# Column sums of a pairwise-product kernel on 64-row halves of the array, with the dense rows written behind the bank copies

## The chip, the cores and the metric

The kernel runs on one core of one Trainium2 chip. The metric is the device time of one execution in microseconds (us); lower is better. In the text PE is the matmul engine (PEld its weight loads), DVE the vector engine, ACT the scalar engine, POOL the engine that issues the gathers, SP the one that issues the other DMAs.

## What is computed

2048 samples each have 32 ids. Every id picks a row of 64 floats from its own table, which makes `e` of shape 2048 x 32 x 64. For each pair of fields i < j (496 pairs) there is a 64 x 64 matrix, and the value of the pair is a bilinear form; a small three-layer network follows, all in float32:

```python
p, q = x[:, row_idx, :], x[:, col_idx, :]          # row_idx, col_idx: the 496 pairs
z = einsum('bpe,fpe,bpf->bp', p, kernel, q)        # 2048 x 496
h = concatenate([z, dense_ctx], axis=1)            # 496 + 16 = 512 columns
h = maximum(h @ W_top1 + b_top1, 0)                # 512 -> 512
h = maximum(h @ W_top2 + b_top2, 0)                # 512 -> 256
y = h @ W_top3                                     # 256 -> 1
```

## The kernel before

The samples are taken in 4 chunks of 512. Within a chunk the samples lie along the free dimension, and the features of two fields (2 x 64) along the 128 partitions.

- **Gather and turn.** POOL gathers rows with indirect DMAs (line 181), 8 for a pair of fields, into a ring of four slots `rows`. PE transposes them (`turn`, line 218) into a side bank, and ACT copies them to `xt`.
- **Duos.** The 496 pairs are handled four at a time; such a group is a duo, 124 in a chunk. Of these 120 are "block" duos: two matmuls, each with a 64x128 weight tile on one half of the array's rows (`bilinear`, lines 270 and 271), which write the two banks of `y_ps`. Four duos of a chunk are "special" (pairs within one block) and use four 64x64 tiles (lines 273 to 276). DVE then multiplies the 128 x 1024 results by the other field's features and writes `products`, a ring of four (line 417).
- **Sums.** Two duos are a quad, 62 in a chunk. `add_up` (line 288) sums the products of a quad over features with a 0/1 matrix `selector` as weights: four matmuls, one per block of 32 output partitions. With the product of a duo's bank as moving operand, partitions 0 to 63 belong to one pair and 64 to 127 to another, so the selector has two columns of ones, and one matmul puts two rows into the bank. A bank of 128 rows (4 x 32) is full after 16 quads (`Z_QUADS`); there are four banks' worth in a chunk (`Z_BANKS`), which alternate between `sum_ps[0]` and `sum_ps[1]`. The last one has only 28 of every 32 rows filled (`SUM_ROWS`); the other 16 rows of `z_sb` hold the dense features.
- **Bank copies.** ACT copies a full bank to `z_sb` (`copy_bank`); the last one of a chunk goes in four copies of 28 rows, so that the dense rows are left alone. While ACT copies one bank, PE sums into the other.
- **Dense rows.** SP writes the dense rows with four DMAs of 4 rows (`place_dense`, line 197), for chunks 0 and 1 at the start, and for chunks 2 and 3 when layer 1 of the chunk that used the same half of `z_sb` is done.
- **Network.** `layer1` (line 231), `layer2` (239) and `layer3` (247) of chunk c are side jobs, placed between the duos of chunk c+1 by `side_schedule`: the first of the four `layer1` jobs stands before duo 6. For the last chunk they run alone behind the last sum.

PE takes its work in program order: side jobs that are due before a duo, the duo, and behind each odd duo the sum of the quad before. Each engine's program is written out by hand and synchronised by semaphores. A float32 matmul appears in the trace as two records (passes), each with a weight load of its own.

The sum before, as it stands in `add_up`:

```python
for m in range(4):
    last = nc.tensor.matmul(sum_ps[kb % 2][32 * m:32 * m + 32, :], selector[:, 30 - 2 * s:62 - 2 * s],
                            products[:, (2 * g + m // 2) % 4, m % 2, :], ...)
```

Of the kernel before, what the change touches and what calls it, by code (L numbers as in the profile page):

```python
# [10 lines left out]
B, F, E = 2048, 32, 64  # L11
DENSE, H1, H2 = 16, 512, 256
P = 128
N = 512
CHUNKS = B // N
# [21 lines left out]
QUADS = DUOS // 2  # L37
FIRST_DUO = {q: DUO.index(("block", 0, q)) for q in range(1, PAIRS)}
SPECIAL_DUO = {u: DUO.index(("special", u, None)) for u in range(SPECIALS)}

Z_QUADS = P // 8
Z_BANKS = -(-QUADS // Z_QUADS)
SUM_ROWS = 2 * (QUADS - (Z_BANKS - 1) * Z_QUADS)

PIECES = [(0, 4)] + [(d, d + 8) for d in range(4, DUOS, 8)]

# [13 lines left out]
def z_rows():  # L60
    rows, dense = [], 0
    for kb in range(Z_BANKS):
        for r in range(P):
            column_tile, s, half = r // 32, r % 32 // 2, r % 2
            quad = kb * Z_QUADS + s
            if quad < QUADS:
                duo = DUO[2 * quad + column_tile // 2]
                rows.append(tuple(sorted(field_pair(duo, column_tile % 2, half))))
            else:
                rows.append(dense)  # L70
                dense += 1
    return rows
# [29 lines left out]
SIDE = {job: k for k, job in enumerate(SIDE_ORDER)}  # L102


def dlrm_tower(nc, ids, tables, pair_kernel, dense, w1, b1, w2, b2, w3, out):
    with ExitStack() as ctx:  # L106
        def psum(name, shape):
            return ctx.enter_context(nc.psum_tensor(name, shape, F32))

        def sem(name):  # L110
            return ctx.enter_context(nc.semaphore(name))

        def sb(name, shape, dt=F32):
            return ctx.enter_context(nc.sbuf_tensor(name, shape, dt))
# [5 lines left out]
        products = sb("products", [P, 4, 2, N])  # L120
        z_sb = sb("z_sb", [P, 2, Z_BANKS, N])
        w1_sb = sb("w1_sb", [P, 4, H1])
# [6 lines left out]
        y_sb = sb("y_sb", [P, N])  # L129
        idx = sb("idx", [P, CHUNKS, TILES, F], I32)  # L130
        identity = sb("identity", [P, P])
        selector = sb("selector", [P, 62])

        y_ps = [psum(f"y_ps{i}", [P, 2, N]) for i in range(2)]
        sum_ps = [psum(f"sum_ps{i}", [P, N]) for i in range(2)]
# [7 lines left out]
        selector_made = sem("selector_made")  # L143
        kernel_landed = [sem(f"kernel_landed{i}") for i in range(len(PIECES))]
        weights_landed = sem("weights_landed")
        dense_landed = [sem(f"dense_landed{c}") for c in range(CHUNKS)]
        side_ready = sem("side_ready")
# [4 lines left out]
        quad_summed = sem("quad_summed")  # L152
        bank_kept = sem("bank_kept")
        out_written = sem("out_written")

        LAST_BANK = Z_BANKS - 1

        def banks_kept(c, kb):

            return c * (Z_BANKS + 3) + (kb + 1 if kb < LAST_BANK else Z_BANKS + 3)  # L160

        block = ctx.enter_context(nc.Block())

# [21 lines left out]
        @block.sync  # L185
        def _(sp):
            sp.dma_start(idx[:, 0], ids[:, 0]).then_inc(ids_landed[0], 16)
            for p, (lo, hi) in enumerate(PIECES):
                sp.dma_start(kernel_sb[:, lo:hi, :], pair_kernel[:, lo:hi, :]).then_inc(kernel_landed[p], 16)
                if p == 3:  # L190
                    sp.dma_start(idx[:, 1:], ids[:, 1:]).then_inc(ids_landed[1], 16)
            for dst, src in ((w1_sb, w1), (w2_sb, w2), (w3_sb, w3), (b1_sb, b1), (b2_sb, b2)):
                sp.dma_start(dst[:], src).then_inc(weights_landed, 16)

            def place_dense(c):
                for g in range(4):
                    sp.dma_start(z_sb[32 * g + SUM_ROWS:32 * g + 32, c % 2, LAST_BANK, :],
                                 dense[4 * g:4 * g + 4, c * N:c * N + N]).then_inc(dense_landed[c], 16)

            place_dense(0)  # L200
            place_dense(1)
            for c in range(CHUNKS):
                if c + 2 < CHUNKS:
                    sp.wait_ge(side_ready, SIDE["layer1", c, 3] + 1)
                    place_dense(c + 2)
                sp.wait_ge(side_kept, SIDE["layer3", c, 0] + 1)
                sp.dma_start(out[:, c * N:c * N + N], y_sb[32 * c:32 * c + 1, :]).then_inc(out_written, 16)
            sp.wait_ge(out_written, CHUNKS * 16)

        @block.tensor  # L210
        def _(pe):
# [10 lines left out]
            def layer1(c, n):  # L222
                k = SIDE["layer1", c, n]
                if n == 0:
                    pe.wait_ge(bank_kept, banks_kept(c, LAST_BANK))
                    pe.wait_ge(dense_landed[c], 4 * 16)
                    if c == 0:
                        pe.wait_ge(weights_landed, 5 * 16)
                pe.wait_ge(side_kept, k - 1)
                for kb in range(4):  # L230
                    last = nc.tensor.matmul(side_ps[k % 2][:], w1_sb[:, kb, n * P:n * P + P], z_sb[:, c % 2, kb, :],  # L231
                                            start=(kb == 0), stop=(kb == 3))
                last.then_inc(side_ready, 1)
# [46 lines left out]
            def add_up(c, quad):  # L280
                g = c * QUADS + quad
                pe.wait_ge(duo_multiplied, 2 * g + 2)
                kb, s = quad // Z_QUADS, quad % Z_QUADS
                if s == 0 and c * Z_BANKS + kb >= 2:
                    free = c * Z_BANKS + kb - 2
                    pe.wait_ge(bank_kept, banks_kept(free // Z_BANKS, free % Z_BANKS))
                for m in range(4):
                    last = nc.tensor.matmul(sum_ps[kb % 2][32 * m:32 * m + 32, :], selector[:, 30 - 2 * s:62 - 2 * s],  # L288
                                            products[:, (2 * g + m // 2) % 4, m % 2, :],
                                            start=(s == 0), stop=(s == Z_QUADS - 1 or quad == QUADS - 1))  # L290
                last.then_inc(quad_summed, 1)

            pe.wait_ge(identity_made, 1)
            pe.wait_ge(selector_made, 2)
            for c in range(CHUNKS):
                stored, pieces = 0, 0
                for d in range(DUOS):
                    for job in SIDE_BEFORE[c, d]:
                        side(job)
                    kind, s, q = DUO[d]  # L300
# [17 lines left out]
        def _(act):  # L318
            def copy(dst, src):
                return nc.scalar.activation(dst, src, ACT.Copy)  # L320
# [47 lines left out]
                copy(special[high, u % 2, 0, :], x[high, 4 * u + 2, :]).then_inc(special_kept, 1)  # L368
                copy(special[low, u % 2, 0, :], x[high, 4 * u + 3, :]).then_inc(special_kept, 1)

            def copy_bank(c, kb):
                act.wait_ge(quad_summed, c * QUADS + min(Z_QUADS * (kb + 1), QUADS))
                if c >= 2 and kb == 0:
                    act.wait_ge(side_ready, SIDE["layer1", c - 2, 3] + 1)
                if kb < LAST_BANK:
                    copy(z_sb[:, c % 2, kb, :], sum_ps[kb % 2][:]).then_inc(bank_kept, 1)
                else:
                    for g in range(4):
                        part = slice(32 * g, 32 * g + SUM_ROWS)
                        copy(z_sb[part, c % 2, kb, :], sum_ps[kb % 2][part, :]).then_inc(bank_kept, 1)  # L380

            for c in range(CHUNKS):
                for d in range(DUOS):
                    for job in SIDE_BEFORE[c, d]:
                        keep(job)
                        if c == 0 and job[0] == "turn" and job[1] == 0 and job[2] % 4 == 3:
                            special_slots(0, job[2] // 4)
                    for u in range(SPECIALS):
                        if c and d == max(0, SPECIAL_DUO[u] - 14):
                            special_slots(c, u)  # L390
                    if d % 2 and d > 2 and (d // 2) % Z_QUADS == 0:
                        copy_bank(c, d // 2 // Z_QUADS - 1)
                    if d == 1 and c:
                        copy_bank(c - 1, LAST_BANK)
            copy_bank(CHUNKS - 1, LAST_BANK)
            for job in SIDE_AFTER:
                keep(job)

        @block.vector
        def _(dve):  # L400
            nc.vector.memset(selector[:], 0.0).then_inc(selector_cleared, 1)
            dve.wait_ge(selector_cleared, 1)
            nc.vector.memset(selector[0:E, 30:31], 1.0).then_inc(selector_made, 1)
            nc.vector.memset(selector[E:P, 31:32], 1.0).then_inc(selector_made, 1)
            for c in range(CHUNKS):
                for d in range(DUOS):
                    g = c * DUOS + d
                    if g >= 4:
                        dve.wait_ge(quad_summed, g // 2 - 1)
                    dve.wait_ge(duo_ready, g + 1)  # L410
                    kind, s, q = DUO[d]
                    if kind == "block":
                        by = xt[:, c % 2, s, :].unsqueeze(1).to_broadcast([P, 2, N])
                    else:
                        dve.wait_ge(special_kept, 4 * (c * SPECIALS + s + 1))
                        by = special[:, s % 2]
                    nc.vector.tensor_tensor(products[:, g % 4], y_ps[g % 2][:], by, ALU.mult).then_inc(duo_multiplied, 1)  # L417
# [45 lines left out]
```

## Time and profile before

| | |
|---|---|
| median of 3 runs | 920.45 us (918.14 to 920.97) |
| profiled execution | 919.69 us, span 917.9 us |
| busy: PE / DVE / POOL / ACT | 94% / 64% / 53% / 12% of the span |
| mean granted clock of TensorE | 0.994 |
| HBM read | 26.91 MB, mean 29 GB/s |
| DVE multiplies | 496 x 1.22 us |
| PE records: y 64x128, sums 128x32 | 1920, 1984 |

The span runs from the first to the last instruction of the profiled execution, whose own time is 1.8 us longer. Busy shares say which engine is full, not what ends the work; for that the waits and the timeline are read. Matmul ends in the trace are modelled and overlap with the next start, so phases of PE are read from start to start. Times of the timeline count from the span's start.

### The profile page before, as it was taken

To read this page: it belongs to the slowest core of one execution; us is meant where nothing else is said; L and a number is where in the kernel's file an instruction comes from. 1 tells how busy PE (TensorE), PEld (TensorE's weight loads), DVE (VectorE), ACT (ScalarE), POOL (GpSimd) and SP (SyncE) were. 2 spreads that over 40 slices of the span, in tenths; PEclk is the share of its full clock that TensorE was granted. 3 is DMA by queue.
4 is the path that set the end of the run, shared out by engine and by line. 5 is a ranking of instruction groups with operands and counts; after the bars stand their busy time and mean duration, and the time that the engine had idled before them with its cause. 6 is when DMAs were issued, how large, how long until landed. Compare 5 with 4: busy or idle time off the path is not lost.

```text
span 917.9 us, 10931 instructions
## 1 busy us (share of the span) xinstructions
PE 864.0 (94%) x4496; PEld 272.8 (30%) x4496; DVE 584.5 (64%) x499; ACT 114.3 (12%) x185; POOL 483.9 (53%) x518
## 2 busy tenths in 40 slices
PE   0189999999999999999999999999999999999988
PEld 0123333332333332333233333333333333222223
DVE  0047777777746558777765656777776566778840
ACT  0011011100211111101112011001111110100012
POOL 6777777777777776677535465567724600000000
PEclk9989999999999999999999999999999999999999
DMA  9411111111111111111100011111100100000000
GB/s 338 148 27 27 28 27 26 28 27 27 27 27 28 28 26 24 24 25 25 21 12 19 18 24 19 21 25 25 25 9 18 22 2 1 0 1 1 1 0 0
DMA packets 19881, 27.64 MB, mean 30 GB/s; under 512 B 9012, under 2 KB 9268, under 8 KB 19704
## 3 DMA queue, kind: packets, MB, share of 16 engines
q0 software_dynamic: 16384, 16.81, 9.4%
q1 hardware_dynamic: 3448, 10.14, 3.0%
q8 instruction: 35, 0.57, 0.3%
q14 instruction: 14, 0.11, 0.0%
HBM read 26.91 MB, written 0.01 MB: 29 GB/s over the span
## 4 chain that ended last, share of the span: by engine, by line
PE 71%; POOL 20%; issue 7%; DMA 0%; ACT 0%; DVEq 0%; DVE 0%; POOLq 0%
PE y_ps L270 37%; POOL rows L181 20%; PE sum_ps L288 20%; PE side_ps L231 6%; PE side_ps L239 3%; PE side_ps L218 3%; PE y_ps L273 1%; PE side_ps L247 1%; PE y_ps L271 1%; DMA rows<-tbl_dram,idx 0%; ACT z_sb L320 0%; DMA idx<-ids_dram 0%; DVEq L106 0%; DVE products L417 0%; ACT h_sb L340 0%
## 5 line engine op out<-in xcount | busy, mean ns | idle before, releaser
L417 DVE TENSOR_TENSOR products<-y_ps,xt 128x1024 f32<-128x1024 f32 x480 | 566.1, 1219 | 281.3 <-PE y_ps L271 281.2
L181 POOL DMA_INDIRECT rows<-tbl_dram,idx x512 | 483.2, 944 | 249.4 <-issue 150.1
L270 PE MATMUL y_ps<-xt,kernel_sb 64*128 64x512 f32 x960 | 481.1, 620 | 0.5 <-DVE products L417 0.4
L271 PE MATMUL y_ps<-xt,kernel_sb 64*128 64x512 f32 x960 | 481.2, 620 | 0.0
L288 PE MATMUL sum_ps<-products,selector 128*32 128x512 f32 x1984 | 264.2, 605 | 0.7 <-DVE products L417 0.7
L270 PEld LDWEIGHTS y_ps<-xt,kernel_sb 64*128 64x128 f32 x960 | 160.2, 187 | 286.8 <-DVE products L417 182.9
L271 PEld LDWEIGHTS y_ps<-xt,kernel_sb 64*128 64x128 f32 x960 | 159.9, 187 | 0.0
L320 ACT ACTIVATE xt<-side_ps 128x512 f32<-128x512 f32 x64 | 38.2, 597 | 503.7 <-PE side_ps L218 479.4
L288 PEld LDWEIGHTS sum_ps<-products,selector 128*32 128x32 f32 x1984 | 39.1, 108 | 189.1 <-issue 187.6
L218 PE MATMUL side_ps<-identity,rows 128*128 128x128 f32 x256 | 44.7, 300 | 46.4 <-DMA rows<-tbl_dram,idx 46.4
L231 PE MATMUL side_ps<-z_sb,w_sb 128*128 128x512 f32 x128 | 59.5, 613 | 2.5 <-ACT z_sb L320 2.5
L218 PEld LDWEIGHTS side_ps<-identity,rows 128*128 128x128 f32 x256 | 28.5, 147 | 98.2 <-issue 60.3
L320 ACT ACTIVATE special<-xt 64x512 f32<-64x512 f32 x64 | 40.1, 627 | 1.6
L320 ACT ACTIVATE z_sb<-sum_ps 28x512 f32<-28x512 f32 (+1 forms) x28 | 16.6, 592 | 190.4 <-PE sum_ps L288 190.1
L231 PEld LDWEIGHTS side_ps<-z_sb,w_sb 128*128 128x128 f32 x128 | 23.9, 195 | 34.0 <-issue 30.5
L417 DVE TENSOR_TENSOR products<-y_ps,special 128x1024 f32<-128x1024 f32 x16 | 19.6, 1222 | 19.1 <-issue 19.1
L239 PE MATMUL side_ps<-h_sb,w_sb 128*128 128x512 f32 x64 | 29.3, 604 | 0.8 <-ACT h_sb L334 0.8
L334 ACT ACTIVATE h_sb<-side_ps,b_sb 128x512 f32<-128x512 f32 x16 | 11.0, 687 | 66.5 <-PE side_ps L231 66.5
L239 PEld LDWEIGHTS side_ps<-h_sb,w_sb 128*128 128x128 f32 x64 | 11.6, 190 | 18.6 <-issue 17.0
L276 PE MATMUL y_ps<-xt,kernel_sb 64*64 64x512 f32 x32 | 17.1, 615 | 0.0
L273 PE MATMUL y_ps<-xt,kernel_sb 64*64 64x512 f32 x32 | 17.1, 615 | 0.0
L274 PE MATMUL y_ps<-xt,kernel_sb 64*64 64x512 f32 x32 | 17.1, 615 | 0.0
(19 smaller groups left out, 48.4 us busy)
## 6 DMA issues: line engine op xcount, KB each, us to landing
rows<-tbl_dram,idx POOLq DMA_INDIRECT x512, 2.4
kernel_sb<-pair_kernel_dram SPq DMA_DIRECT2D x15, 512.0 KB, 11.0
w_sb<-w_dram SPq DMA_DIRECT2D x1, 1024.0 KB, 18.2
w_sb<-w_dram SPq DMA_DIRECT2D x1, 512.0 KB, 18.1
kernel_sb<-pair_kernel_dram SPq DMA_DIRECT2D x1, 256.0 KB, 2.8
z_sb<-dense_dram SPq DMA_DIRECT2D x16, 8.0 KB
idx<-ids_dram SPq DMA_DIRECT2D x1, 192.0 KB, 6.9
idx<-ids_dram SPq DMA_DIRECT2D x1, 64.0 KB, 1.9
```

The source lines that it names most:

```text
L181: pool.indirect_dma_start(rows[:, slot, t, h, :], None, tables[j], bass.IndirectOffsetOnAxis(ap=idx[:, c, t, j:j + 1], axis=0)).then_inc(r ...
L218: last = nc.tensor.transpose(side_ps[k % 2][:, t * P:(t + 1) * P], rows[:, q % ROW_RING, t].rearrange("p h e -> p (h e)"), identity[:])
L231: last = nc.tensor.matmul(side_ps[k % 2][:], w1_sb[:, kb, n * P:n * P + P], z_sb[:, c % 2, kb, :], start=(kb == 0), stop=(kb == 3))
L239: last = nc.tensor.matmul(side_ps[k % 2][:], w2_sb[:, kb, n * P:n * P + P], h1_sb[:, kb, :], start=(kb == 0), stop=(kb == 3))
L270: nc.tensor.matmul(y[:, 0, :], kernel_sb[low, d, :], x[low, q, :], start=True, stop=True)
L271: last = nc.tensor.matmul(y[:, 1, :], kernel_sb[high, d, :], x[high, q, :], start=True, stop=True)
L273: nc.tensor.matmul(y[low, 0, :], kernel_sb[low, d, low], x[low, 4 * s + 3, :], start=True, stop=True)
L274: nc.tensor.matmul(y[low, 1, :], kernel_sb[high, d, low], x[high, 4 * s, :], start=True, stop=True)
L276: last = nc.tensor.matmul(y[high, 1, :], kernel_sb[high, d, high], x[high, 4 * s + 1, :], start=True, stop=True)
L288: last = nc.tensor.matmul(sum_ps[kb % 2][32 * m:32 * m + 32, :], selector[:, 30 - 2 * s:62 - 2 * s], products[:, (2 * g + m // 2) % 4, m % ...
L320: return nc.scalar.activation(dst, src, ACT.Copy)
L417: nc.vector.tensor_tensor(products[:, g % 4], y_ps[g % 2][:], by, ALU.mult).then_inc(duo_multiplied, 1)
```

## The change

Each matmul of the sum is split in two along the rows: partitions 0 to 63 and 64 to 127 are separate 64x32 tiles, each with one column of ones, and each half of the rows has a bank of its own (`sum_ps[half]`). A quad now takes eight matmuls, and a pair of banks fills over 32 quads (`Z_QUADS = P // 4`). Both banks of a pair are copied together, by two whole copies, and the first sum of the next pair waits for both. In a chunk's last pair 30 of every 32 rows are sums. The copies now cover all 128 rows, so the dense rows can only be written behind them: SP waits until all copies of the chunk are done and then issues eight DMAs of 2 rows; `layer1` waits for these. The rows of the first weight matrix are permuted on the host to match.

```diff
-Z_QUADS = P // 8
-Z_BANKS = -(-QUADS // Z_QUADS)
-SUM_ROWS = 2 * (QUADS - (Z_BANKS - 1) * Z_QUADS)
+Z_QUADS = P // 4
+Z_BANKS = 2 * -(-QUADS // Z_QUADS)
+SUM_ROWS = QUADS % Z_QUADS
...
-            def place_dense(c):
-                for g in range(4):
-                    sp.dma_start(z_sb[32 * g + SUM_ROWS:32 * g + 32, c % 2, LAST_BANK, :],
-                                 dense[4 * g:4 * g + 4, c * N:c * N + N]).then_inc(dense_landed[c], 16)
-
-            place_dense(0)
-            place_dense(1)
             for c in range(CHUNKS):
-                if c + 2 < CHUNKS:
-                    sp.wait_ge(side_ready, SIDE["layer1", c, 3] + 1)
-                    place_dense(c + 2)
+                sp.wait_ge(bank_kept, (c + 1) * Z_BANKS)
+                for kb in range(Z_BANKS - 2, Z_BANKS):
+                    for g in range(4):
+                        row = 8 * (kb - Z_BANKS + 2) + 2 * g
+                        sp.dma_start(z_sb[32 * g + SUM_ROWS:32 * g + 32, c % 2, kb, :],
+                                     dense[row:row + 2, c * N:c * N + N]).then_inc(dense_landed[c], 16)
...
                 if n == 0:
-                    pe.wait_ge(bank_kept, banks_kept(c, LAST_BANK))
-                    pe.wait_ge(dense_landed[c], 4 * 16)
+                    pe.wait_ge(dense_landed[c], 8 * 16)
...
-                kb, s = quad // Z_QUADS, quad % Z_QUADS
-                if s == 0 and c * Z_BANKS + kb >= 2:
-                    free = c * Z_BANKS + kb - 2
-                    pe.wait_ge(bank_kept, banks_kept(free // Z_BANKS, free % Z_BANKS))
+                kb, s = quad // Z_QUADS * 2, quad % Z_QUADS
+                if s == 0 and c * Z_BANKS + kb:
+                    pe.wait_ge(bank_kept, c * Z_BANKS + kb)
                 for m in range(4):
-                    last = nc.tensor.matmul(sum_ps[kb % 2][32 * m:32 * m + 32, :], selector[:, 30 - 2 * s:62 - 2 * s],
-                                            products[:, (2 * g + m // 2) % 4, m % 2, :],
-                                            start=(s == 0), stop=(s == Z_QUADS - 1 or quad == QUADS - 1))
+                    for half in range(2):
+                        part = slice(half * E, half * E + E)
+                        last = nc.tensor.matmul(sum_ps[half][32 * m:32 * m + 32, :], selector[part, 31 - s:63 - s],
+                                                products[part, (2 * g + m // 2) % 4, m % 2, :],
+                                                start=(s == 0), stop=(s == Z_QUADS - 1 or quad == QUADS - 1))
                 last.then_inc(quad_summed, 1)
...
-                if kb < LAST_BANK:
-                    copy(z_sb[:, c % 2, kb, :], sum_ps[kb % 2][:]).then_inc(bank_kept, 1)
-                else:
-                    for g in range(4):
-                        part = slice(32 * g, 32 * g + SUM_ROWS)
-                        copy(z_sb[part, c % 2, kb, :], sum_ps[kb % 2][part, :]).then_inc(bank_kept, 1)
+                for half in range(2):
+                    copy(z_sb[:, c % 2, kb + half, :], sum_ps[half][:]).then_inc(bank_kept, 1)
...
-            nc.vector.memset(selector[0:E, 30:31], 1.0).then_inc(selector_made, 1)
-            nc.vector.memset(selector[E:P, 31:32], 1.0).then_inc(selector_made, 1)
+            nc.vector.memset(selector[:, 31:32], 1.0).then_inc(selector_made, 1)
```

How the instructions stand now. On PE, in one quad of chunk 1 (y matmuls of two duos, then the sum), before:

```order
L270 MATMUL y_ps<-xt,kernel_sb 128x512 [waits duo_multiplied]
L271 MATMUL y_ps<-xt,kernel_sb 128x512
L270 MATMUL y_ps<-xt,kernel_sb 128x512 [waits duo_multiplied]
L271 MATMUL y_ps<-xt,kernel_sb 128x512
L288 MATMUL sum_ps<-products,selector 32x512 [waits duo_multiplied]
L288 MATMUL sum_ps<-products,selector 32x512 x3
```

and after:

```order
L259 MATMUL y_ps<-xt,kernel_sb 128x512 [waits duo_multiplied]
L260 MATMUL y_ps<-xt,kernel_sb 128x512
L259 MATMUL y_ps<-xt,kernel_sb 128x512 [waits duo_multiplied]
L260 MATMUL y_ps<-xt,kernel_sb 128x512
L278 MATMUL sum_ps<-products,selector 32x512 [waits duo_multiplied]
L278 MATMUL sum_ps<-products,selector 32x512 x7
```

The order is the same; the sum has eight matmuls in place of four.

On SP, behind the weights, before:

```order
L197 DMA z_sb<-dense_dram 4x512 x8
L197 DMA z_sb<-dense_dram 4x512 [waits side_ready]
L197 DMA z_sb<-dense_dram 4x512 x3
L207 DMA out_dram<-y_sb 1x512 [waits side_kept]
```

and after:

```order
L194 DMA z_sb<-dense_dram 2x512 [waits bank_kept]
L194 DMA z_sb<-dense_dram 2x512 x7
L197 DMA out_dram<-y_sb 1x512 [waits side_kept]
L194 DMA z_sb<-dense_dram 2x512 [waits bank_kept]
L194 DMA z_sb<-dense_dram 2x512 x7
```

Each chunk has eight issues, and they stand behind that chunk's bank copies.

On ACT, at the end of the program, before:

```order
L320 ACTIVATE special<-xt 64x512 x3
L320 ACTIVATE z_sb<-sum_ps 28x512 [waits quad_summed]
L320 ACTIVATE z_sb<-sum_ps 28x512 x3
L334 ACTIVATE h_sb<-side_ps,b_sb 128x512 [waits side_ready] x4
```

and after:

```order
L310 ACTIVATE special<-xt 64x512 x3
L310 ACTIVATE z_sb<-sum_ps 128x512 [waits quad_summed]
L310 ACTIVATE z_sb<-sum_ps 128x512
L324 ACTIVATE h_sb<-side_ps,b_sb 128x512 [waits side_ready] x4
```

Two whole copies stand where four of 28 rows stood.

## Rows read from the trace of the kernel before

**Rows 1.** The page: busy time by engine, us (share of the span) xinstructions.
```profile
PE 864.0 (94%) x4496; PEld 272.8 (30%) x4496; DVE 584.5 (64%) x499; ACT 114.3 (12%) x185; POOL 483.9 (53%) x518
```

**Rows 2.** Waits of PE, then POOL, 75 to 254 us: total, times, longest.
```profile
PE side_ps L218 <- DMA rows<-tbl_dram,idx: 1.5, 2, 0.9
POOL rows L181 <- issue: 44.2, 145, 0.3
```

**Rows 3.** Waits of PE from 258 us to the end.
```profile
PE side_ps L231 <- ACT z_sb L320: 2.5, 1, 2.5
PE side_ps L247 <- ACT h_sb L340: 0.8, 1, 0.8
PE side_ps L239 <- ACT h_sb L334: 0.8, 1, 0.8
PE sum_ps L288 <- DVE products L417: 0.7, 1, 0.7
```

**Rows 4.** Timeline, 502 to 505 us: start, us, engine, line, operation.
```profile
502.24 0.59 PE L270 MATMUL y_ps<-xt,kernel_sb 64*128 64x512 f32 x1
...
502.76 1.07 PE L288 MATMUL sum_ps<-products,selector 128*32 128x512 f32 x8
503.76 0.18 PEld L270 LDWEIGHTS y_ps<-xt,kernel_sb 64*128 64x128 f32 x1 [0.84 <-DVE products L417]
...
504.29 0.59 PE L270 MATMUL y_ps<-xt,kernel_sb 64*128 64x512 f32 x1
...
504.72 0.59 PE L270 MATMUL y_ps<-xt,kernel_sb 64*128 64x512 f32 x1
```

**Rows 5.** Timeline, 306 to 308 us, around a special duo.
```profile
306.09 0.59 PE L271 MATMUL y_ps<-xt,kernel_sb 64*128 64x512 f32 x1
...
306.60 0.13 PEld L273 LDWEIGHTS y_ps<-xt,kernel_sb 64*64 64x64 f32 x1 [0.76 <-DVE products L417]
...
306.66 0.13 PEld L273 LDWEIGHTS y_ps<-xt,kernel_sb 64*64 64x64 f32 x1
...
306.68 0.13 PEld L276 LDWEIGHTS y_ps<-xt,kernel_sb 64*64 64x64 f32 x1
...
307.62 0.16 PEld L288 LDWEIGHTS sum_ps<-products,selector 128*32 128x32 f32 x8 [0.81 <-issue]
```

**Rows 6.** Line 288 by stretch: its length, PE busy (records), PEld busy (records), clock.
```profile
254.00:886.90 632.90, 197.11 (x1480) 29.16 (x1480) 1.00 0.09 17
75.00:254.00 179.00, 61.02 (x460) 8.99 (x456) 1.00 0.14 27
```

**Rows 7.** Timeline of the end.
```profile
886.97 2.42 ACT L320 ACTIVATE z_sb<-sum_ps 28x512 f32<-28x512 f32 x4 [36.56 <-PE sum_ps L288]
...
889.44 15.70 PE L231 MATMUL side_ps<-z_sb,w_sb 128*128 128x512 f32 x32 [2.54 <-ACT z_sb L320]
```

**Rows 8.** Timeline where chunk 1 ends, 465 to 472 us.
```profile
465.06 2.43 ACT L320 ACTIVATE z_sb<-sum_ps 28x512 f32<-28x512 f32 x4 [20.29 <-PE sum_ps L288]
...
466.84 1.07 PE L288 MATMUL sum_ps<-products,selector 128*32 128x512 f32 x8
...
471.33 1.55 PE L231 MATMUL side_ps<-z_sb,w_sb 128*128 128x512 f32 x3
```

**Rows 9.** Timeline of SP's issues: four dense pieces, and the last output.
```profile
299.82 1.26 SPq L197 DMA_DIRECT2D z_sb<-dense_dram  x4
...
916.38 0.23 SPq L207 DMA_DIRECT2D out_dram<-y_sb  x1
```

**Rows 10.** The page: DMA issues, KB each, us from issue to landing.
```profile
kernel_sb<-pair_kernel_dram SPq DMA_DIRECT2D x1, 256.0 KB, 2.8
...
idx<-ids_dram SPq DMA_DIRECT2D x1, 64.0 KB, 1.9
```

**Rows 11.** All engines by stretch at the end, with the granted clock.
```profile
890.40:893.80 3.40, 3.40 (x5) 1.33 (x4) 0.00 (x0) 0.00 (x0) 0.00 (x0) 0.50 0.00 0
893.80:918.00 24.20, 20.38 (x47) 8.09 (x45) 0.00 (x0) 4.71 (x7) 0.00 (x0) 1.00 0.00 0
```

More of the change, by code:

```diff
@@ L63, in z_rows @@
         for r in range(P):
-            column_tile, s, half = r // 32, r % 32 // 2, r % 2
-            quad = kb * Z_QUADS + s
+            column_tile, s, half = r // 32, r % 32, kb % 2
+            quad = kb // 2 * Z_QUADS + s
             if quad < QUADS:
@@ L131, in dlrm_tower @@
         identity = sb("identity", [P, P])
-        selector = sb("selector", [P, 62])
+        selector = sb("selector", [P, 63])
         y_ps = [psum(f"y_ps{i}", [P, 2, N]) for i in range(2)]
@@ L154, in dlrm_tower @@
         out_written = sem("out_written")
-        LAST_BANK = Z_BANKS - 1
-        def banks_kept(c, kb):
-            return c * (Z_BANKS + 3) + (kb + 1 if kb < LAST_BANK else Z_BANKS + 3)
         block = ctx.enter_context(nc.Block())
@@ L282, in add_up @@
                 pe.wait_ge(duo_multiplied, 2 * g + 2)
-                kb, s = quad // Z_QUADS, quad % Z_QUADS
-                if s == 0 and c * Z_BANKS + kb >= 2:
-                    free = c * Z_BANKS + kb - 2
-                    pe.wait_ge(bank_kept, banks_kept(free // Z_BANKS, free % Z_BANKS))
+                kb, s = quad // Z_QUADS * 2, quad % Z_QUADS
+                if s == 0 and c * Z_BANKS + kb:
+                    pe.wait_ge(bank_kept, c * Z_BANKS + kb)
                 for m in range(4):
-                    last = nc.tensor.matmul(sum_ps[kb % 2][32 * m:32 * m + 32, :], selector[:, 30 - 2 * s:62 - 2 * s],
-                                            products[:, (2 * g + m // 2) % 4, m % 2, :],
-                                            start=(s == 0), stop=(s == Z_QUADS - 1 or quad == QUADS - 1))
+                    for half in range(2):
[3 more added lines that the diff above has]
+                                                start=(s == 0), stop=(s == Z_QUADS - 1 or quad == QUADS - 1))
                 last.then_inc(quad_summed, 1)
             pe.wait_ge(identity_made, 1)
-            pe.wait_ge(selector_made, 2)
+            pe.wait_ge(selector_made, 1)
             for c in range(CHUNKS):
@@ L369, in special_slots, with copy_banks @@
                 copy(special[low, u % 2, 0, :], x[high, 4 * u + 3, :]).then_inc(special_kept, 1)
-            def copy_bank(c, kb):
-                act.wait_ge(quad_summed, c * QUADS + min(Z_QUADS * (kb + 1), QUADS))
+            def copy_banks(c, kb):
+                act.wait_ge(quad_summed, c * QUADS + min(Z_QUADS * (kb // 2 + 1), QUADS))
                 if c >= 2 and kb == 0:
                     act.wait_ge(side_ready, SIDE["layer1", c - 2, 3] + 1)
-                if kb < LAST_BANK:
-                    copy(z_sb[:, c % 2, kb, :], sum_ps[kb % 2][:]).then_inc(bank_kept, 1)
-                else:
-                    for g in range(4):
-                        part = slice(32 * g, 32 * g + SUM_ROWS)
-                        copy(z_sb[part, c % 2, kb, :], sum_ps[kb % 2][part, :]).then_inc(bank_kept, 1)
+                for half in range(2):
+                    copy(z_sb[:, c % 2, kb + half, :], sum_ps[half][:]).then_inc(bank_kept, 1)
             for c in range(CHUNKS):
@@ L391, in _ @@
                     if d % 2 and d > 2 and (d // 2) % Z_QUADS == 0:
-                        copy_bank(c, d // 2 // Z_QUADS - 1)
+                        copy_banks(c, 2 * (d // 2 // Z_QUADS - 1))
                     if d == 1 and c:
-                        copy_bank(c - 1, LAST_BANK)
-            copy_bank(CHUNKS - 1, LAST_BANK)
+                        copy_banks(c - 1, Z_BANKS - 2)
+            copy_banks(CHUNKS - 1, Z_BANKS - 2)
             for job in SIDE_AFTER:
```

## The prediction

> **What bounds the kernel now.** I read the page's busy shares first: PE is busy for 94% of the span, DVE for 64%, ACT for 12% [rows 1]. A busy share alone does not say who sets the end, so the next view is who waited for whom, cut at the point where the kinds of wait change. From 75 to 254 us PE waits 1.5 us in all, both times in a turn for gathered rows, while POOL waits for nobody but its own issue [rows 2]: in this stretch the gather sets the pace and PE keeps just behind it. From 258 us on PE waits for another engine only four times, 4.8 us in all, and all of it in the last 33 us [rows 3]. So every microsecond that is added to PE's stream between 254 and 887 us is a microsecond of the time, and what is added before 254 us is partly eaten by the 1.5 us of waiting.
>
> Next the timeline of one quad of the steady state [rows 4]. Starts are 0.43 us apart while y matmuls follow each other (504.29 and 504.72). From the last y start at 502.24 to the first sum start it is 0.52, and from the last sum start (first at 502.76, and the phase is over at 503.76) again some 0.52. So the array is empty for about 0.09 us at each change of the tile's form, and the first weight load behind it is not hidden. The whole sum phase, from its first weight load to the next y's, takes 503.76 - 502.76 = 1.00 us, of which two passes are 2 x 0.43 = 0.86.
>
> Is it the change from 64-row to 128-row tiles that empties the array? Four duos of a chunk are "special": 64x64 tiles between 64x128 ones and sums. There the row height stays at 64 and only the columns change, and from the last 64x128 start (306.09) to the first 64x64 load (306.60) it is 0.51 to 0.52 us, as everywhere else [rows 5]. So a change of columns alone already costs the same gap. After the edit the sums are 64x32 between 64x128 tiles: the column width still changes. I expect both gaps to stay.
>
> **The change part by part.** (a) *Eight matmuls for four in each quad.* The sum of a quad moves the same columns: all 128 rows and all 128 columns of the array are covered by eight 64x32 tiles as by four 128x32. If the eight run side by side, the two passes stay 0.86 us. What grows is the stagger: in the special duo the first of the four second loads starts at 306.66 and the fourth at 306.68, so one start takes about 0.02/3 = 0.0067 us [rows 5]. The phase ends with the last tile, hence four more starts add 4 x 0.0067 = 0.027 us to a quad. A check on the same rows: the special phase (four tiles, 64-column load) is 307.62 - 306.60 = 1.02 against 1.00 for the sum (four tiles, 32-column load of half the length), so phases are the sum of load, two passes, stagger and gap. From 254 us to the end 1480 sum records are 185 quads of eight [rows 6]; the very last one waits 0.7 us for DVE anyway [rows 3], which leaves 184. 184 x 0.027 = **+4.9 us**. In the stretch before 254 us 460 records are 57 quads, 57 x 0.027 = 1.5, as much as the 1.5 us that PE waits there for rows [rows 2, 6]: nothing. The rows are rounded to 0.01, which leaves 0.005 to 0.008 us a start and 3.7 to 5.9 for the term. It is 0 if the starts hide behind the pass; its upper bound is that only four tiles run at a time: one more pass of 0.43 a quad (a rival below).
> In a sentence of its own: the Trainium skill, page "TensorE: Matmul & The Clock Gate", section "Measured speedup vs the span model", has a pack's span as one matmul plus about 4 ns for each further tile; by that the term would be 184 x 4 x 0.004 = 2.9 us, an estimate. The row of this trace (6.7 ns) is the one I use.
>
> (b) *Bank hand-over.* Before, bank k is copied while the other one fills. Now both banks of a pair fill together and the next quad must wait for both copies. At a chunk's end the four copies of today begin at 465.06, take 2.43 together, so 0.61 each, and the next sum starts at 466.84 [rows 8]; two copies end at 465.06 + 1.21 = 466.27. Spare: 0.57 us, seven times in the kernel, and ACT (12% busy) has nothing else due there: **0**. If that cover were gone, it would be at most 7 x 0.6 = 4 us.
>
> (c) *Dense rows behind the copies.* Three of the four chunks have cover. SP may issue from 466.27 on. One issue of a 4-row piece takes 1.26/4, hence with the pause between two about 0.33 us [rows 9]; eight are 7 x 0.33 = 2.3. The landing of such a small one has no time in the trace; the 64 KB load of the indices lands after 1.9, the 256 KB piece of the kernel after 2.8, and the 2 KB output ends the program 917.9 - 916.38 = 1.5 after its issue at most [rows 9, 10]. I take 1.8, near the larger. Then the dense rows are there at 466.3 + 2.3 + 1.8 = 470.4, and layer 1 starts at 471.33 [rows 8]: 0.9 us spare, **0**. If it fails, PE stands and with it the duos queued behind layer 1: 3 times up to about 1 us.
> The last chunk has no cover. Now: ACT starts at 886.97, four copies of 28 rows take 2.42, layer 1 begins at 889.44 [rows 7]. After: two copies end at 886.97 + 1.21 = 888.18, the last of eight issues is at +2.3 = 890.5, landed at +1.8 = 892.3. Layer 1 at 892.35 in place of 889.44: **+2.9 us**. Bounds: landing 1.5 to 2.8, an issue 0.25 to 0.4, so +2.0 to +4.4.
>
> (d) *PE's clock at the end.* After today's 2.54 us of idle PE [rows 7] the granted clock falls to 0.50 from 890.4 to 893.8, and is 1.00 again after it [rows 11]; that stretch of 3.4 us costs 1.7 us. After the edit the idle stretch is 5.5 us. The half clock may then fall partly into the idle time (cheaper) or last longer (dearer). I book **0**, with -1.0 to +1.7 as bounds.
>
> (e) *The small ones.* Copies go from 28 to 16 and the first eight dense writes leave SP's start, where no one waited for them; the selector is one memset fewer; PE reads 992 more matmul instructions, and its queue was ahead, since the four starts of a pack follow at 0.0067. All 0. On SP the dense writes of a chunk now stand behind the output of the chunk before, which follows layer 3 before duo 46, long before the copies at the chunk's end.
>
> Sum: 4.9 + 0 + 0 + 2.9 + 0 = +7.8 us against the profiled execution (919.69, span 917.9): 927.5. The median of the runs shown, 920.45, is 0.8 above the profiled one, so the forecast is **928.0**.
>
> **The rivals.**
> *A, only four tiles at a time* (chance 0.08). No row shows more than four tiles side by side: y has two, special and sum four. If the fifth has to wait for a second pass to begin, a quad takes one pass more, 0.43 us: 184 x 0.43 = 79, plus 57 x 0.43 - 1.5 = 23 before 254 us, plus 2.9, on 920.45: about 1025 us. Against it speaks that four tiles in a 2 by 2 arrangement behave like four in a row [rows 5]. The Trainium skill, same page, section "Measured speedup vs the span model", lists sixteen 32x32 tiles at once; no run here shows it.
> *B, faster: the gap is tied to row height after all* (0.03). It is one mechanism, at both ends of each sum: without a change of rows the array would not be emptied, and a quad would save 2 x 0.09 of gap plus the exposed load (the first two starts of y are 504.29 - 503.76 = 0.53 apart, 0.10 over a pass [rows 4]) = 0.28. It decides as soon as it exceeds (7.8/184) = 0.04 a quad. 184 x 0.28 = 52 less, with the tail's 2.9 more: 872 us; POOL would not stop it, it waits for PE from 254 us on. Against it speaks the 0.51 at the special duo [rows 5].
> *C, nothing measurable* (0.05): the starts hide, the tail costs 2 us or the clock falls into the idle time: 920.5 to 923.
> *D, the covers of (b) or (c) are too thin* (0.09): as forecast plus 3 to 6 us, 931 to 934.
>
> **How the numbers follow.** The forecast has 0.75. Its own range: term (a) 3.7 to 5.9, tail 2.0 to 4.4, clock -1.0 to +1.7, all against 920.45, gives 925 to 932. With D and part of C the range 922 to 935 holds the time in 8 to 9 of 10 cases; rival A and B stay out. A measurement of this kernel tells about 0.3% (2.8 us) from no change, that is 917.7 to 923.2. Slower by more: forecast, A, D = 0.92. Within: C = 0.05. Faster: B = 0.03.
>
> **What would show it.** In the profile after: 3968 records of 64x32 sums with starts some 7 ns apart, all eight first passes before any second one; a sum phase of 1.02 to 1.03 us in place of 1.00; the gaps of 0.52 unchanged; no PE wait for ACT at the first sum of a pair; one PE wait of 5 to 6 us before the last layer 1, with a DMA as what ended it, and eight issues on SP inside it. The prediction is wrong if the sum phase is near 1.4 us (A) or under 0.95 us (B), or if PE waits for z_sb at the chunks' borders (D).

## The result, and the profile after

The changed kernel takes 927.45 us (median of 4 runs, 927.07 to 930.25) against 920.31 for the kernel before on the same chip; the ratio is 1.0088, 95% interval 1.0062 to 1.0114. It is 7.1 us slower. The forecast was 928.0, range 922 to 935.

The profiled execution of the changed kernel is the longest of its four, 930.25 us with a span of 928.5, so 2.8 us above the median; where it differs from the others is told below. First a steady quad, from the timeline (start, us, engine, line, operation); it answers to [rows 4]:

```profile
507.07 0.59 PE L260 MATMUL y_ps<-xt,kernel_sb 64*128 64x512 f32 x1
...
507.59 0.18 PEld L278 LDWEIGHTS sum_ps<-products,selector 64*32 64x32 f32 x16 [0.76 <-issue]
507.59 1.09 PE L278 MATMUL sum_ps<-products,selector 64*32 64x512 f32 x16
508.61 0.18 PEld L259 LDWEIGHTS y_ps<-xt,kernel_sb 64*128 64x128 f32 x1 [0.84 <-DVE products L402]
```

All sixteen records of a sum lie within 1.09 us, so eight tiles run side by side: a quad has no third or fourth pass. The phase from the first sum load to the next y load is 508.61 - 507.59 = 1.02 us against 1.00. The gap ahead of it (from the last y start to the first sum start) is 507.59 - 507.07 = 0.52 as before.

Single rows are rounded to 0.01 us, too coarse for 0.02 a quad. The starts of the first layer 1 job in chunks 2 and 3 are 62 quads apart, with the same side jobs between them in both kernels, and serve as marks. Here they are from PE's timeline, first of the kernel before:

```profile
471.33 1.13 PE L231 MATMUL side_ps<-z_sb,w_sb 128*128 128x512 f32 x2
...
685.22 1.13 PE L231 MATMUL side_ps<-z_sb,w_sb 128*128 128x512 f32 x2
```

and of the changed one:

```profile
476.02 0.70 PE L220 MATMUL side_ps<-z_sb,w_sb 128*128 128x512 f32 x1
...
691.37 1.12 PE L220 MATMUL side_ps<-z_sb,w_sb 128*128 128x512 f32 x2
```

That is 213.89 against 215.35 us: 1.46 more for 62 quads, 0.0235 us a quad. Over the 184 quads that PE paces it makes 4.3 us. The figure repeats: the profiles of the three kernels with the old sums (before, runs 2 and 7) have 213.89 us, those of the six with eight tiles (after, runs 1, 4, 5, 6 and 8) 215.33 to 215.35.

In the nanoseconds that the traces hold, the starts of a sum's tiles follow each other by 6.7 ns on average in both kernels. Four more of them are 27 ns. The gap behind the sum, from its last start to the next y start, is 4 ns shorter (519 in place of 523 ns, medians over the steady stretch), which leaves 23. Ahead of the sum it is 518 to 520 ns in both.

Where a chunk ends, the timeline of the changed kernel answers to [rows 8]:

```profile
469.74 1.08 ACT L310 ACTIVATE z_sb<-sum_ps 128x512 f32<-128x512 f32 x2 [20.52 <-PE sum_ps L278]
...
470.85 2.31 SPq L194 DMA_DIRECT2D z_sb<-dense_dram  x8
...
471.48 1.09 PE L278 MATMUL sum_ps<-products,selector 64*32 64x512 f32 x16
```

The two copies are done at 470.82, 0.66 us before the first sum of the next pair, and the eight issues at 473.16, 2.9 us before layer 1 at 476.02 (the second fence of marks). PE waits for neither. What PE waits for from 256 us on (total, times, longest) shows that the dense rows cost something in one place alone; it answers to [rows 3]:

```profile
PE side_ps L220 <- DMA z_sb<-dense_dram: 4.7, 1, 4.7
PE side_ps L228 <- ACT h_sb L324: 0.8, 1, 0.8
PE side_ps L236 <- ACT h_sb L330: 0.8, 1, 0.8
PE sum_ps L278 <- DVE products L402: 0.7, 1, 0.7
```

And the end, from the timeline and from the table by stretch (length, busy time of PE, PEld, DVE, ACT, POOL with their records, then the granted clock), which answer to [rows 7, 11]:

```profile
894.54 1.08 ACT L310 ACTIVATE z_sb<-sum_ps 128x512 f32<-128x512 f32 x2 [83.54 <-PE sum_ps L278]
895.65 2.31 SPq L194 DMA_DIRECT2D z_sb<-dense_dram  x8
...
899.17 9.23 PE L220 MATMUL side_ps<-z_sb,w_sb 128*128 128x512 f32 x15 [4.73 <-DMA z_sb<-dense_dram]
```

```profile
897.40:904.20 6.80, 5.03 (x6) 2.19 (x7) 0.00 (x0) 0.00 (x0) 0.00 (x0) 0.50 0.02 3
904.40:928.00 23.60, 20.33 (x47) 8.05 (x45) 0.00 (x0) 4.71 (x7) 0.00 (x0) 1.00 0.00 0
255.80:259.10 3.30, 3.30 (x12) 1.42 (x10) 0.54 (x1) 0.60 (x1) 2.40 (x3) 0.50 0.13 27
```

ACT's first copy starts 4.63 us before layer 1 (899.17 - 894.54) against 2.47 before (889.44 - 886.97): +2.2 us. The half clock now lasts 6.8 us, of which PE works 5.0; before it was 3.4 with PE at work all the time. So it costs 2.5 in place of 1.7 us. From the start of layer 1 to the end of the span it is 29.3 us here and 28.5 before, and 26.8 in runs 1 and 8, whose clock stays up. The last row is a half clock of its own in the middle, right behind a wait for gathered rows:

```profile
255.51 0.93 PE L208 MATMUL side_ps<-identity,rows 128*128 128x128 f32 x4 [1.89 <-DMA rows<-tbl_dram,idx]
```

The kernel before waited 0.58 us at that turn and its clock stayed up. In the profiled runs of the other kernels with these sums (waits of at most 1.5 us there) the clock stays up too. The half clock costs 1.7 us, and the longer wait 1.3. Together they are about the profiled execution's surplus over its median; the other three executions have no trace, but run 4, which does the same work, reaches this layer 1 at 257.60 in place of 260.67 and takes 926.92 us.

The account of that profile: +3.2 us until the first layer 1 (257.45 before, 260.67 after: the gather's longer wait and the half clock behind it), +1.46 a chunk for two chunks, +1.4 for the 60 quads from the last of these marks to ACT's copies (894.54 - 691.37 against 886.97 - 685.22), +2.2 from ACT's first copy to layer 1, +0.9 in the clock. Together 10.6, the difference of the spans.

### The profile page after: what moved, and what is told of

It reads as the page before. It is cut to its first block, busy times and chain, and to the rows that moved or that the text cites. A ratio compares the mean times of both kernels' runs of the same rounds, so it can differ in the third digit from the quotient of the medians.

```text
span 928.5 us, 14894 instructions
## 1 busy us (share of the span) xinstructions
PE 870.9 (94%) x6480; PEld 279.0 (30%) x6480; DVE 585.3 (63%) x498; ACT 106.4 (11%) x173; POOL 483.9 (52%) x518
## 4 chain that ended last, share of the span: by engine, by line
PE 71%; POOL 20%; issue 7%; DMA 1%; ACT 0%; SPq 0%; DVEq 0%; DVE 0%; POOLq 0%
PE y_ps L259 36%; POOL rows L175 20%; PE sum_ps L278 20%; PE side_ps L220 6%; PE side_ps L228 3%; PE side_ps L208 3%; PE y_ps L262 1%; PE side_ps L236 1%; PE y_ps L260 1%; DMA rows<-tbl_dram,idx 0%; DMA idx<-ids_dram 0%; SPq L194 0%; DVEq L106 0%; DMA z_sb<-dense_dram 0%; ACT z_sb L310 0%
## 5 line engine op out<-in xcount | busy, mean ns | idle before, releaser
L278 PE MATMUL sum_ps<-products,selector 64*32 64x512 f32 x3968 | 270.2, 601 | 0.7 <-DVE products L402 0.7
L278 PEld LDWEIGHTS sum_ps<-products,selector 64*32 64x32 f32 x3968 | 45.0, 105 | 189.4 <-issue 187.8
L228 PE MATMUL side_ps<-h_sb,w_sb 128*128 128x512 f32 x64 | 29.3, 604 | 0.8 <-ACT h_sb L324 0.8
L310 ACT ACTIVATE z_sb<-sum_ps 128x512 f32<-128x512 f32 x16 | 8.7, 595 | 163.7 <-PE sum_ps L278 163.7
```

The lines of the kernel that those rows point to most:

```text
L228: last = nc.tensor.matmul(side_ps[k % 2][:], w2_sb[:, kb, n * P:n * P + P], h1_sb[:, kb, :], start=(kb == 0), stop=(kb == 3))
L278: last = nc.tensor.matmul(sum_ps[half][32 * m:32 * m + 32, :], selector[part, 31 - s:63 - s], products[part, (2 * g + m // 2) % 4, m % 2, ...
```

## The experiments

Theory S is the forecast: four more starts in each sum on the stretch that PE paces, and the dense writes behind the last copies, with the clock. Theory T puts the whole loss at the end. Each ratio is against the kernel before on the same chip; a difference between two changed kernels is one of medians that can come from different chips, and is read together with the traces.

**1. Without the dense writes.**

```diff
-                sp.wait_ge(bank_kept, (c + 1) * Z_BANKS)
-                for kb in range(Z_BANKS - 2, Z_BANKS):
...
-                        sp.dma_start(z_sb[32 * g + SUM_ROWS:32 * g + 32, c % 2, kb, :],
-                                     dense[row:row + 2, c * N:c * N + N]).then_inc(dense_landed[c], 16)
...
-                    pe.wait_ge(dense_landed[c], 8 * 16)
+                    pe.wait_ge(bank_kept, (c + 1) * Z_BANKS)
```

> The changed kernel without its dense writes; layer 1 waits for the bank copies alone (the 16 dense columns are left out of the network's input). Theory S (my forecast: four more starts in each sum, 23 ns a quad on the stretch that PE sets, and the dense writes behind the last copies): the end loses the DMA wait, 5.3 us from the last sum's start to layer 1 becomes about 2, and the clock falls for a shorter time; time near 923, that is still 3 us above the kernel before. Theory T (the sums are free, the whole loss is the tail and the clock behind it): 919 or less. Sum phases stay 1.02 us under S.

Measured: 922.05 us, ratio 1.0030 (1.0018 to 1.0042). The wait at the end (PE's waits and timeline) is short:

```profile
PE side_ps L214 <- ACT z_sb L304: 1.2, 1, 1.2
```

```profile
890.82 1.09 PE L272 MATMUL sum_ps<-products,selector 64*32 64x512 f32 x16 [0.65 <-DVE products L396]
892.01 1.08 ACT L304 ACTIVATE z_sb<-sum_ps 128x512 f32<-128x512 f32 x2 [83.53 <-PE sum_ps L272]
...
893.15 2.41 PE L214 MATMUL side_ps<-z_sb,w_sb 128*128 128x512 f32 x5 [1.24 <-ACT z_sb L304]
```

The table by stretch has the clock at full to the end; it was expected to fall for a shorter time:

```profile
893.00:919.00 26.00, 23.04 (x52) 9.31 (x52) 0.00 (x0) 4.81 (x8) 0.00 (x0) 1.00 0.00 0
```

So the late dense rows are worth about 5.4 us of the changed kernel's 7.1. Left are 2.2 us against the kernel before, although two copies are now faster than four (1.3 us less wait) and the clock does not fall at the end (1.7 less). So something costs 5.2 us: the sums 4.3 by the marks (the chunk is 215.35 us here too), and in this profile the part ahead of the first layer 1 is 0.7 longer, where the three profiles with the old sums differ by 1.3 among themselves. Theory T, with 919 or less, falls.

**2. The dense rows late, the sums as before.** `place_dense` issues eight DMAs of 2 rows here.

```diff
-            place_dense(0)
-            place_dense(1)
...
             for c in range(CHUNKS):
...
+                sp.wait_ge(bank_kept, (c + 1) * Z_BANKS)
+                place_dense(c)
...
-                if kb < LAST_BANK:
-                    copy(z_sb[:, c % 2, kb, :], sum_ps[kb % 2][:]).then_inc(bank_kept, 1)
-                else:
...
+                copy(z_sb[:, c % 2, kb, :], sum_ps[kb % 2][:]).then_inc(bank_kept, 1)
```

> The kernel before with four 128x32 sums, but its last bank copied whole and the dense rows written behind the copy by eight DMAs of 2 rows. Theory S: stretches between the chunks' first layer 1 starts stay 213.9 us; from the last sum's start to layer 1 it grows from 3.1 to about 4.7 us (one copy less than in the changed kernel, the same eight issues); time 922 to 923.5. Theory T: the same loss as in the changed kernel, 927. If the dense writes have cover everywhere: 919, since three copies fewer stand in the tail.

Measured: 922.25 us, ratio 1.0026 (1.0012 to 1.0040), as S has it. The marks of chunks 2 and 3 and the end, from the timeline:

```profile
472.11 1.13 PE L230 MATMUL side_ps<-z_sb,w_sb 128*128 128x512 f32 x2
...
685.99 0.70 PE L230 MATMUL side_ps<-z_sb,w_sb 128*128 128x512 f32 x1
...
887.74 0.60 ACT L319 ACTIVATE z_sb<-sum_ps 128x512 f32<-128x512 f32 x1 [36.56 <-PE sum_ps L287]
888.36 2.31 SPq L199 DMA_DIRECT2D z_sb<-dense_dram  x8
...
892.01 1.96 PE L230 MATMUL side_ps<-z_sb,w_sb 128*128 128x512 f32 x2 [4.34 <-issue]
```

The chunk is back at 213.88 us with the old sums. Runs 1 and 2 thus each hold one part of the loss, and the chunk's length follows the sums, not the place of the dense writes. From ACT's copy to layer 1 it is 4.27 us, 1.8 more than before (from the first start of the last sum it is 5.4 against 3.6; the 4.7 and 3.1 of the expectation are counted from some 0.5 us later). The half clock behind this wait lasts 3.4 us, as in the kernel before, and not 6.8 as in the changed one.

**3. Sums in the form of the y matmuls.**

```diff
-                        last = nc.tensor.matmul(sum_ps[half][32 * m:32 * m + 32, :], selector[part, 31 - s:63 - s],
+                        at = 127 - 32 * m - s
+                        last = nc.tensor.matmul(sum_ps[half][:], selector[part, at:at + P],
                                                 products[part, (2 * g + m // 2) % 4, m % 2, :],
-                                                start=(s == 0), stop=(s == Z_QUADS - 1 or quad == QUADS - 1))
+                                                start=(s == 0 and m == 0),
+                                                stop=(m == 3 and (s == Z_QUADS - 1 or quad == QUADS - 1))
```

> The changed kernel with each sum in 64x128 tiles, the form of the y matmuls: the four column blocks run one behind the other through a 255-column selector, so a sum takes four times its passes (8 x 0.43 = 3.4 us) and the time is near 1450. Looked at for the gap alone. If the gap comes from the change of the tile's form, the last y start and the first sum start are 0.43 us apart and the first weight load is hidden. If it comes from the change of bank, from accumulation or from the wait on DVE, it stays at 0.52.

Measured: one run, 1483.7 us, where near 1450 was expected; the difference was not followed up. The 16 records of a quad's sum take 3.60 us. The timeline at a border of y and sum:

```profile
503.12 0.59 PE L259 MATMUL y_ps<-xt,kernel_sb 64*128 64x512 f32 x1
503.12 0.19 PEld L279 LDWEIGHTS sum_ps<-products,selector 64*128 64x128 f32 x2 [0.23 <-issue]
503.12 0.59 PE L260 MATMUL y_ps<-xt,kernel_sb 64*128 64x512 f32 x1
...
503.55 3.60 PE L279 MATMUL sum_ps<-products,selector 64*128 64x512 f32 x16
```

The sum starts 0.43 us behind the last y, and its weights are loaded during that y pass (503.12). The banks, the accumulation and the semaphore are as in the changed kernel; the form of the tile is equal now (and with it only two tiles run side by side), and the gap is gone, behind the sum too. So it is the change of form that empties the array. That tells why the edit could not gain: 64x128 to 64x32 is such a change as much as 64x128 to 128x32.

A change of rows alone has a price of its own. It stands in the trace of the kernel before, where the last pass of a layer 1 job (128x128) is followed by a y matmul (64x128) that waits for nobody:

```profile
500.32 0.59 PE L231 MATMUL side_ps<-z_sb,w_sb 128*128 128x512 f32 x1
500.84 0.69 PE L270 MATMUL y_ps<-xt,kernel_sb 64*128 64x512 f32 x1
```

That is 0.52 us again. So columns alone (the special duos), rows alone, and both together cost the same 0.09 us, to within 4 ns: 519 ns from start to start behind 64-row tiles, 522 or 523 behind 128-row ones.

**4. The other order of the eight.**

```diff
-                for m in range(4):
-                    for half in range(2):
+                for half in range(2):
+                    for m in range(4):
```

> The changed kernel with the eight matmuls of a sum in another order: four column blocks of the lower rows, then four of the upper ones. Theory S (tiles run side by side, only the starts are in line): no difference, 927, the eighth start 0.05 us behind the first. If row halves pair up, or if two tiles of one column block hold each other: a sum phase away from 1.02 us and a time away by more than 3 us.

Measured: 927.28 us, ratio 1.0090 (1.0074 to 1.0106), the same as the changed kernel. The marks of chunks 2 and 3:

```profile
472.94 1.13 PE L220 MATMUL side_ps<-z_sb,w_sb 128*128 128x512 f32 x2
...
688.27 0.70 PE L220 MATMUL side_ps<-z_sb,w_sb 128*128 128x512 f32 x1
```

215.33 us: the tiles do not disturb each other in either order.

**5. Dense issues on two queues.** ACT issues four of the eight behind its copies.

```diff
-                for kb in range(Z_BANKS - 2, Z_BANKS):
+                for kb in range(Z_BANKS - 2, Z_BANKS - 1):
...
+                if kb == Z_BANKS - 2:
+                    act.wait_ge(bank_kept, (c + 1) * Z_BANKS)
+                    for g in range(4):
+                        act.dma_start(z_sb[32 * g + SUM_ROWS:32 * g + 32, c % 2, Z_BANKS - 1, :],
+                                      dense[8 + 2 * g:10 + 2 * g, c * N:c * N + N]).then_inc(dense_landed[c], 16)
```

> The changed kernel with the eight dense issues split: SP issues four, ACT the other four behind its own copies. If the eight issues in line on SP are part of the tail (0.34 us each), the wait before the last layer 1 shrinks by about 4 x 0.34 = 1.3 us, to near 3.4, and the time by 1 to 3 us (the clock goes with it). If only the landing counts, the wait stays 4.7.

Measured: 926.41 us, ratio 1.0071 (1.0057 to 1.0085). SP's and ACT's issues and the wait:

```profile
893.75 1.12 SPq L194 DMA_DIRECT2D z_sb<-dense_dram  x4
893.75 1.23 ACTq L370 DMA_DIRECT2D z_sb<-dense_dram  x4
...
896.44 9.09 PE L220 MATMUL side_ps<-z_sb,w_sb 128*128 128x512 f32 x15 [3.91 <-DMA z_sb<-dense_dram]
```

The issues take half the time (1.2 for 2.31), and the wait shrinks by 0.8 of the expected 1.3 us. Part of the miss is the price of an issue: eight in line start 0.30 us apart, not 0.34, so four of them are worth 1.2. The median is 1.0 us lower, which the two intervals do not tell from nothing; the wait in the trace is the firmer figure. The half clock stays (0.50 from 894.5 to 901.2). Why another 0.3 us of the saving comes back in the landing is not settled; 1.5 us pass from the end of the issues to layer 1 here, 1.2 in the changed kernel.

**6. Layer 1 starts with its finished banks, in the changed kernel.**

```diff
                 if n == 0:
-                    pe.wait_ge(dense_landed[c], 8 * 16)
+                    pe.wait_ge(bank_kept, c * Z_BANKS + 2)
...
                 for kb in range(4):
+                    if n == 0 and kb == 2:
+                        pe.wait_ge(dense_landed[c], 8 * 16)
```

> The changed kernel, but layer 1 begins with the two banks that were copied 30 quads earlier and waits for the dense writes only before its third one. Two of the four weight blocks (2 x 0.86 = 1.7 us) then run inside the wait. Theory S (the tail is a plain wait on PE): 1.7 us less, and more if the clock stays up for longer; 924 to 926. If the wait only moves behind the two blocks and the clock falls as before: 926. If it were not the wait that costs: 927.

Measured: 924.47 us, ratio 1.0045 (1.0030 to 1.0059). The wait is 3.0 in place of 4.7 us, just the two blocks less, in the timeline of the end; the half clock lasts 3.4 in place of 6.8 us (the second fence, the table by stretch). From the last sum's start to the end of the span it is 2.4 us less than in the changed kernel; the other 0.6 of the 3.0 between the medians lies in the spread of the runs.

```profile
891.93 1.98 PE L222 MATMUL side_ps<-z_sb,w_sb 128*128 128x512 f32 x4
...
896.87 6.68 PE L222 MATMUL side_ps<-z_sb,w_sb 128*128 128x512 f32 x11 [2.95 <-DMA z_sb<-dense_dram]
```

```profile
897.20:900.60 3.40, 3.40 (x5) 1.35 (x4) 0.00 (x0) 0.20 (x1) 0.00 (x0) 0.50 0.00 0
900.70:922.00 21.30, 19.19 (x44) 7.50 (x42) 0.00 (x0) 4.34 (x7) 0.00 (x0) 1.00 0.00 0
```

**7. The same in the kernel before.** Layer 1 waits for its last bank only before the fourth block.

```diff
-                    pe.wait_ge(bank_kept, banks_kept(c, LAST_BANK))
-                    pe.wait_ge(dense_landed[c], 4 * 16)
+                    pe.wait_ge(bank_kept, banks_kept(c, LAST_BANK - 1))
...
                 for kb in range(4):
+                    if n == 0 and kb == LAST_BANK:
+                        pe.wait_ge(bank_kept, banks_kept(c, LAST_BANK))
+                        pe.wait_ge(dense_landed[c], 4 * 16)
```

> The kernel before with the same idea: layer 1 starts with its three finished banks and waits for the last one before the fourth block. 3 x 0.86 = 2.6 us of work cover the 2.5 us wait for ACT's four copies, and the clock has no idle stretch to fall behind. Time 920.3 - 2.5 - 1.7 = 916, under both kernels. If the clock falls all the same: 917.8.

Measured: 916.65 us, ratio 0.9960 (0.9946 to 0.9975). It beats both kernels. The end in its timeline, and its clock by stretch:

```profile
887.10 1.07 PE L290 MATMUL sum_ps<-products,selector 128*32 128x512 f32 x8 [0.67 <-DVE products L419]
...
888.10 9.32 PE L233 MATMUL side_ps<-z_sb,w_sb 128*128 128x512 f32 x21
888.24 2.42 ACT L322 ACTIVATE z_sb<-sum_ps 28x512 f32<-28x512 f32 x4 [36.56 <-PE sum_ps L290]
```

```profile
885.00:914.00 29.00, 25.50 (x71) 9.54 (x68) 2.05 (x2) 7.06 (x11) 0.00 (x0) 1.00 0.00 0
```

Layer 1 follows the last sum without a wait while ACT copies, and the granted clock is 1.00 throughout. Expected were 916. In the two profiles the part from the last sum's start to the end is 4.3 us shorter, as expected; the medians are 3.3 apart, and the first layer 1 is 1.3 us later in this profile.

**8. The wait filled with work of no use.**

```diff
             add_up(CHUNKS - 1, QUADS - 1)
+            for _ in range(5):
+                nc.tensor.matmul(y_ps[0][:, 0, :], w1_sb[:, 0, 0:P], w1_sb[:, 1, :], start=True, stop=True)
```

> The changed kernel with five 128x512 matmuls of no use (into a y bank that nobody reads any more) in the wait before the last layer 1; they take 5 x 0.86 = 4.3 us, less than the wait. If the idle time of PE is what lets the clock fall, the granted clock stays 1.00 to the end and the time drops by what the half clock costs behind the wait, 0.9 to 2.6 us, to 925 to 926.5. If the clock falls for another reason, 927 to 928.

Measured: 925.16 us, ratio 1.0061 (1.0047 to 1.0076), 2.3 us under the changed kernel.

```profile
891.16 4.56 PE L305 MATMUL y_ps<-w_sb 128*128 128x512 f32 x10
...
895.91 6.28 PE L220 MATMUL side_ps<-z_sb,w_sb 128*128 128x512 f32 x14 [0.18 <-DMA z_sb<-dense_dram]
```

```profile
888.00:922.00 34.00, 30.11 (x98) 11.49 (x94) 2.08 (x2) 5.80 (x9) 0.00 (x0) 1.00 0.01 2
```

The dense rows come no sooner, but the clock stays at 1.00. From the start of layer 1 to the end of the span it is 26.8 us in place of 29.3 (899.17 to 928.5), just the 2.5 us that the half clock cost; the median falls by 2.3. So the clock's fall is a cost of the wait, on top of its length, and goes with PE's idleness.

## Why the prediction was right

- **The stage that PE paces.** Right. The chunk grows by 1.46 us with the new sums and by nothing with the old ones (run 2). Before it, the forecast put 57 quads at nothing. The first layer 1 starts at 257.4 to 258.7 us in the three profiles with the old sums and at 257.5 to 258.8 in five of the six with the new ones, so nothing is seen of them; but 1.3 us would be as large as this spread, so that the gather's wait absorbs them is not shown.
- **(a) Stagger.** Forecast 0.027 a quad and 4.9 us in all; measured 0.0235 and 4.3. The start of 6.7 ns was right; the 4 ns that the gap behind the sum gives back were not foreseen. Rival A is excluded by the sum phase of 1.02 us, rival B by the unchanged gap, and run 3 shows its ground.
  The Trainium skill, page "TensorE: Matmul & The Clock Gate", section "Measured speedup vs the span model", has about 4 ns for a further tile, by which the term was estimated at 2.9 us; this case's trace has 6.7 ns and 4.3 us, and the measurement decides.
- **(b) Hand-over.** Right: no wait, 0.66 us spare where 0.57 was forecast.
- **(c) Dense rows.** Covered in three chunks, as said, with some 1.6 us to spare where 0.9 was forecast (the issues are done 2.9 us before layer 1, and at the end 1.2 us pass from the last issue to layer 1). At the end +2.9 was forecast and +2.2 measured. All three terms were a little long: the two copies took 1.08 us, not 1.21; the last of the eight issues starts 2.05 us after the first, not 2.3 (all eight take 2.31 with the last one's own 0.25); and from that start to layer 1 it was about 1.5, not 1.8.
- **(d) Clock.** Booked at 0, it cost 0.9 more in the profiled run, inside the bounds. Run 8 puts the whole price of the half clock at 2.3 us by the medians and 2.5 by the traces; 1.7 of it the kernel before pays too.
- **The sum.** The terms (a) and (c) were too large by 1.3 us together, and (d) too small by 0.9. That they nearly cancel is luck, so 928.0 is nearer to 927.45 than its parts are. The last step is rounded down as well: 920.45 + 7.8 is 928.25.

## What to carry to other kernels

A change of the tile's form costs the array its overlap whichever side changes, rows or columns (0.09 us each time here); to save it, equal forms must stand next to each other, and making one side equal brings nothing. Splitting a matmul into more concurrent tiles costs the start of each, 6 to 7 ns here, which counts when hundreds of groups follow each other on the engine that sets the pace. A write that must follow the last result costs its full issue and landing once, at the end; look there first for finished inputs with which the next layer can begin, as run 7 does.

## What the runs showed of the hardware that was not expected

- The fall of the clock is a second price of an idle stretch: 1.9 us of waiting for rows was followed by 3.3 us at half clock in one run, 0.58 us at the same turn was not; and 1.24 us of waiting before layer 1 (run 1) left it at 1.00. The length of the wait does not give the length of the half clock: 2.5 us (before), 4.3 (run 2) and 3.0 (run 6) brought 3.4 us of it, while 3.9 (run 5) and 4.7 (after) brought 6.7 and 6.8.
- Two issuing queues in place of one halved the time of the issues (2.31 to 1.2 us) but brought only 0.8 of 1.1 us to the waiting engine.
- Eight tiles accumulate into two banks on all 128 partitions at once with no slowing: passes stay 0.43 us, and the order of the eight makes no difference (215.33 against 215.35 us a chunk, run 4).
